# Second layer of a sparse two-layer graph network: tiles in a new order, all row gathers ahead of the accumulating output writes

## The chip, the cores and the metric

The kernel runs on one core of a Trainium2 chip. The metric is the device time of one execution in microseconds (us); less is better.

## What is computed

The input is x, 2048 rows of 512 numbers, and a random 0/1 matrix adj of 2048 x 2048 with about two ones in a row. The reference, cut:

```python
h = jnp.maximum(_layernorm(x, axis=-1), 0.0)
x = x + _L0_gnn_ref(h, adj, ...)   # 16 heads, scores only where adj is 1, projection, elu
h = jnp.maximum(_layernorm(x, axis=-1), 0.0)
x = x + _L1_gnn_ref(h, adj, ...)

def _L1_gnn_ref(sent_embed, adj_tensor, W_q, b_q, W_k, b_k, W_v, b_v):
    q = sent_embed @ W_q.T + b_q
    k = sent_embed @ W_k.T + b_k
    v = sent_embed @ W_v.T + b_v
    z = scale * (q @ k.T)
    spare_z = z * adj_tensor
    spare_z = jnp.where(spare_z == 0.0, -10000.0, spare_z)
    attn = jax.nn.softmax(spare_z, axis=1)
    return jax.nn.relu(attn @ v)
```

In the second layer every entry without an edge has the score -10000. So a row's attention is a common weight e0 for all 2048 rows plus corrections for its few neighbours.

## The kernel before, in words

**Ranking and tiles.** The kernel first sorts the 2048 rows by their number of neighbours and cuts them into 16 tiles of 128 rows. All rows of a tile have room for the same number of neighbours, the tile's *slots* (`SLOTS`). In the kernel's numbering tiles 0 to 3 have 1 slot each, tile 4 none, and tiles 5 to 15 have 8, 2, 5, 2, 4, 2, 3, 2, 3, 2, 3: 40 slots in all. A slot costs one *gather*: an indirect DMA, issued by GpSimd, that fetches for each of the tile's 128 rows one neighbour's row of 512 numbers.

**First layer.** It goes through the tiles in the order `SEQ`. For each, VectorE forms the hidden rows from gathered neighbours (`aggregate`), TensorE transposes and projects them, VectorE adds the input (`residual`, result in `x1[:, position, :]`), GpSimd takes the power for the normalisation (L1242) and writes x1 into the output tensor (L1243), and ScalarE makes the normalised rows `h_t` (L1115), which go to DRAM as `h1_dram` from the Sync queue (L1186). Between these steps GpSimd's queue issues gathers and loads of x by the tables `GATHER` and `X_LATE`. TensorE transposes h_t (L1334) and multiplies it with the joined query-key matrix: the *query products* (`queries`, L1344 and L1347), copied by ScalarE into `u_all` (`copy_u`).

**Second layer.** Six pieces per tile:

- GpSimd gathers the neighbours' normalised rows, one per slot (`gather1`, L1254). Where they land says `row(k)`: 20 places in `shared`, then 16 in `x1`, then `w_out`.
- VectorE forms one dot product per slot of u and the gathered row (`dot`, L985), then for a group of tiles the scores (`scores1`, L1004 to L1009); ScalarE exponentiates (`exp_scores1`, L1142 and L1143); VectorE normalises (`normalise1`, L1016 to L1023).
- ScalarE writes the *base row*, e0 times the sum of all normalised rows, into one of four buffers `hb` (`base_of`, L1135, for the tile without slots L1137, with the constant 1/N). It waits until the transposes of the tile four before have read that buffer.
- VectorE adds each gathered row times its weight to it (`aggregate1`, L1029, one instruction per slot).
- TensorE transposes the result (`transposes1`, L1388), ScalarE copies it (L1163), TensorE multiplies it with the value matrix into one of four banks (`products`, L1399 and L1401).
- ScalarE applies relu into one of four buffers `o_t` (`output`, L1150), and GpSimd adds these rows in DRAM to the output tensor, an accumulating indirect DMA, here called a *put* (`put`, L1259). ScalarE waits before it writes a buffer for the put that used it four tiles before.

The tiles come in the order 0 to 15, in the groups (0 to 4), (5, 6), (7, 8), (9, 10, 11), (12 to 15), and VectorE has a group's dot products behind the adds of the group before. Nothing schedules this work but the order in which it is written for each engine, each of which runs its instructions in order and waits on semaphores. On GpSimd stand nine tiles of gathers, then put and gathers by turns:

```python
for t in range(9):
    gather1(t)
for t in range(T):
    put(t)
    if 9 + t < T:
        gather1(9 + t)
```

## Time and profile before

| | us |
|---|---|
| median of 3 runs (lowest to highest) | 469.98 (469.42 to 470.12) |
| profiled execution, its own time | 469.46 |
| profiled execution, span from the first to the last instruction | 467.5 |
| TensorE busy | 395.3 (85%) |
| VectorE busy | 369.1 (79%) |
| ScalarE busy | 246.1 (53%) |
| GpSimd busy | 257.9 (55%) |

Of the span the first 205 us or so are the ranking, the input projections and the work on rows with no neighbour; the first layer's tile loop takes the next 140; the second layer runs from about 345 to the end. An engine's busy share is an average over these stages. In the profile PE is TensorE, DVE VectorE, ACT ScalarE, POOL GpSimd; L numbers are lines of the kernel.

### The profile page before, as it was taken

How to read it: one execution, taken by the hardware profiler on the slowest of the kernel's cores; microseconds unless marked ns; L12 is line 12 of the kernel's file. 1: busy time of each engine (PE TensorE's matmuls, PEld its weight loads, DVE VectorE, ACT ScalarE, POOL GpSimd, SP SyncE). 2: the span in 40 equal slices, each digit the busy share in tenths (PEclk: the TensorE clock that was granted, in tenths of full speed). 3: DMA queues.
4: the chain of work that ended last, by engine and by line, in shares of the span. 5: the costliest groups of instructions: out<-in, count | busy, mean ns of one | idle time of the engine just before them, and what ended most of it. 6: DMA issues, size and time to landing. Idle time of an engine off the chain costs nothing.

```text
span 467.5 us, 6241 instructions
## 1 busy us (share of the span) xinstructions
PE 395.3 (85%) x2058; PEld 282.6 (60%) x2070; DVE 369.1 (79%) x731; ACT 246.1 (53%) x511; POOL 257.9 (55%) x268
## 2 busy tenths in 40 slices
PE   7999999997899998989959879789891998866960
PEld 3888887784777887865737546456581565423430
DVE  4999999987899999977999996898445789957300
ACT  4389777766899998924424433444432433312310
POOL 2335241242788677766757648835337787871330
PEclk9599999999899999999989998899996899995995
DMA  8989998510000123445535527632136678873451
GB/s 315 399 320 332 390 339 299 201 70 2 6 6 5 23 72 92 104 126 182 188 87 166 162 91 205 197 122 91 46 113 192 199 174 168 165 162 43 52 65 19
DMA packets 26997, 70.02 MB, mean 150 GB/s; under 512 B 7893, under 2 KB 8149, under 8 KB 24789
## 3 DMA queue, kind: packets, MB, share of 16 engines
q0 software_dynamic: 13056, 38.45, 31.5%
q1 hardware_dynamic: 13904, 31.16, 18.3%
q8 instruction: 17, 0.28, 0.2%
q14 instruction: 16, 0.12, 0.1%
q10 hardware_dynamic: 4, 0.00, 0.0%
HBM read 52.47 MB, written 17.13 MB: 149 GB/s over the span
## 4 chain that ended last, share of the span: by engine, by line
POOL 31%; PE 15%; issue 15%; DVE 9%; DMA 1%; ACT 1%; DVEq 0%; POOLq 0%
PE psum L1303 8%; POOL s_shared L1231 7%; PE psum L1401 5%; POOL s_shared L1254 4%; POOL out_dram L1243 4%; POOL s_x L1254 4%; POOL s_shared L1212 3%; POOL s_rs L1242 3%; POOL out_dram L1259 3%; DVE s_shared L796 2%; DVE s_shared L794 2%; POOL s_x L1249 2%; DVE s_x L810 1%; DMA w_out<-h_dram,s_near_rank 1%; POOL w_out L1254 1%
## 5 line engine op out<-in xcount | busy, mean ns | idle before, releaser
L1064 ACT ACTIVATE s_shared<-psum,seq_all 128x320 bf16<-128x320 f32 x192 | 81.7, 568 | 6.1 <-PE psum L1303 4.4
L1303 PE MATMUL psum<-s_shared 128*128 128x198 bf16 x768 | 75.2, 254 | 9.6 <-POOL s_shared L1212 9.6
L1303 PEld LDWEIGHTS psum<-s_shared 128*128 128x128 bf16 x768 | 67.9, 98 | 17.4 <-POOL s_shared L1212 9.9
L555 PE MATMUL psum<-w_seq,hT 128*128 128x272 f32 x256 | 63.8, 405 | 0.4 <-ACT w_seq L416 0.4
L1325 PE MATMUL psum<-w_out,hT 128*128 128x512 f32 x128 | 60.7, 619 | 0.4
L555 PEld LDWEIGHTS psum<-w_seq,hT 128*128 128x128 f32 x256 | 49.4, 197 | 10.3 <-ACT w_seq L416 0.5
L1347 PE MATMUL psum<-w_qk,s_early 128*128 128x257 f32 x240 | 54.5, 379 | 0.0
L1347 PEld LDWEIGHTS psum<-w_qk,s_early 128*128 128x128 f32 x240 | 44.4, 190 | 6.0
L1231 POOL DMA_INDIRECT s_shared<-seq_dram,tab x30 | 37.7, 1255 | 11.3 <-issue 8.9
L1325 PEld LDWEIGHTS psum<-w_out,hT 128*128 128x128 f32 x128 | 26.0, 203 | 25.8 <-issue 24.9
L1212 POOL TENSOR_TENSOR s_shared<-s_shared 128x1056 f32<-128x1056 f32 x16 | 31.1, 1945 | 15.2 <-DVE s_shared L796 15.2
L274 POOL TENSOR_TENSOR rstd<-veps,power 128x1 f32<-128x1 f32 x16 | 8.9, 558 | 55.2 <-DVE veps L460 55.2
L472 DVE MAX8 near<-adj_ring 128x8 f32<-128x2048 f32 x16 | 36.5, 2284 | 0.6 <-DMA adj_ring<-in_adj_dram 0.6
L475 DVE FIND_INDEX8 tab<-near,adj_ring 128x8 uint32<-128x2048 f32 x16 | 36.6, 2285 | 0.0
L1242 POOL TENSOR_TENSOR s_rs<-s_ve,power 128x1 f32<-128x1 f32 x16 | 13.7, 855 | 38.7 <-DVE s_ve L898 38.6
L1115 ACT ACTIVATE h_t<-s_x,s_nm,s_rs 128x512 f32<-128x512 f32 x16 | 13.1, 816 | 36.5 <-DVE s_nm L905 36.5
L1401 PE MATMUL psum<-wv_t,hT 128*128 128x512 f32 x64 | 31.5, 639 | 0.8 <-ACT hT L1163 0.5
L1259 POOL DMA_INDIRECT out_dram<-s_lone,tab x12 | 19.4, 1619 | 20.6 <-ACT s_lone L1150 18.4
L803 DVE TENSOR_SCALAR s_shared<-psum,neg_s 128x320 bf16<-128x320 f32 x64 | 30.7, 541 | 0.0
L372 ACT ACTIVATE squares<-adj_ring 128x2048 bf16<-128x2048 f32 x16 | 30.4, 1897 | 0.0
L1401 PE MATMUL psum<-wv_t,bout_bc 128*128 128x512 f32 x64 | 28.8, 593 | 0.1
L1254 POOL DMA_INDIRECT s_shared<-h_dram,s_near_rank x20 | 20.6, 1028 | 9.0 <-issue 5.8
(264 smaller groups left out, 756.8 us busy)
## 6 DMA issues: line engine op xcount, KB each, us to landing
adj_ring<-in_adj_dram SPq DMA_DIRECT2D x16, 1024.0 KB, 8.1
seq_dram<-seq_all POOLq DMA_DIRECT2D x16, 264.0 KB, 4.7
x_ring<-in_x_dram SPq DMA_DIRECT2D x16, 256.0 KB, 8.4
h_dram<-h_t SPq DMA_DIRECT2D x16, 256.0 KB, 2.4
w_seq<-in_L_gnn_W_seq_dram SPq DMA_DIRECT2D x1, 1024.0 KB, 5.7
w_q<-in_L_gnn_W_q_dram SPq DMA_DIRECT2D x1, 1024.0 KB, 13.7
w_k<-in_L_gnn_W_k_dram SPq DMA_DIRECT2D x1, 1024.0 KB, 15.9
w_v<-in_L_gnn_W_v_dram SPq DMA_DIRECT2D x1, 1024.0 KB, 9.0
```

Source lines behind the costliest of these rows:

```text
L472: step(dve.max(near[:, t, :], adj_ring[:, t % AR, :]))
L475: dve.max_index(record[:, t, 0:TOP], near[:, t, :], adj_ring[:, t % AR, :]).then_inc(adj_searched, 1)
L555: last = pe.matmul(bank[2 + 2 * (t % 2) + i][:, 0:SX // 2], hT[:, t % 2, c * P:(c + 1) * P], w_seq[:, c, i * (SX // 2):(i + 1) * (SX // 2) ...
L1064: last = act.activation(ind[i][:, j, PAD:], bank[4 + i][:, 0:LN], ACT.Sign, bias=seq_all[:, j, D + n:D + n + 1])
L1212: pool.tensor_tensor(split[i][:, :, 2, :], split[i][:, :, 1, :], top_half(split[i][:, :, 1, :]), ALU.subtract).then_inc(r2_done, 1)
L1231: pool.indirect_dma_start(G(t)[:, s, :], None, seq_dram[:, :], bass.IndirectOffsetOnAxis(tab[:, t, s:s + 1], 0)).then_inc(got[t], 16)
L1254: pool.indirect_dma_start(row(FIRST_SLOT[t] + s), None, h1_dram[:, :], bass.IndirectOffsetOnAxis(near_rank[:, FIRST_SLOT[t] + s:FIRST_SLOT ...
L1259: pool.indirect_dma_start(out[:, :], bass.IndirectOffsetOnAxis(own[:, t, :], 0), o_t[t % 4], None, compute_op=ALU.add).then_inc(out_stored ...
L1303: last = pe.matmul(acc(i)[:, k, 0:3 * W2], ind[i][:, j, k * P:(k + 1) * P], rhs.rearrange("p t w -> p (t w)"), start=(j == 0 and k != 1), ...
L1325: last = pe.matmul(bank[2 + k % 2], hidT[k % 2][:, c * P:(c + 1) * P], w_out[:, c, :], start=False, stop=(c == C - 1))
L1347: last = pe.matmul(bank[u_bank(t) + i][:, 0:hi - lo], h1T(t)[:, c * P:(c + 1) * P], w_qk[:, c, lo:hi], start=False, stop=(c == C - 1))
L1401: last = pe.matmul(bank[2 + t % 4], aT[t % 2][:, c * P:(c + 1) * P], wv_t[:, c, :], start=False, stop=(c == C - 1))
```

## The change

Line numbers in this section are the changed kernel's where the text says so.

- **Tile order.** The second layer takes the tiles in the order `SEQ1` = 4, 0, 1, 2, 3, 6, 8, 10, 12, 14, 11, 13, 15, 9, 7, 5. The groups are now (0 to 3), (6, 8, 10), (12, 14), (9, 11, 13, 15), (5, 7). VectorE's order is written out by hand: dot products of later tiles stand between the adds of earlier ones.
- **GpSimd.** All 40 gathers stand ahead of all 16 puts, with one wait ahead of the 29th and one ahead of the 37th, whose targets are read by earlier work.
- **Places.** Gathered rows no longer use x1: 20 places in `shared`, 4 in `w_out`, 3 in `lone`, 1 in `bv_bc`, 8 in `early`, and the first four places again. ScalarE writes the relued rows into x1, at the tile's own position, and the puts read them there. The wait for an earlier put goes; instead ScalarE waits until all rows of x1 are stored. (`STORED` is 16, so `BY_DVE` is empty and every output goes this way.)
- **TensorE.** The query products of tiles 12 to 14 in `SEQ` order follow the sum of all normalised rows (before, one stood ahead of it, one behind, and the last two between the second layer's tiles); the last stands behind the first transposes. The banks of the query products alternate for all tiles.
- **ScalarE.** Exponentials, waits for weights and base rows are put by the tables `EXP1_AT`, `WEIGHTS_AT`, `BASES_AT`; an output now comes two tiles behind its copy, before one.
- **First layer.** GpSimd gathers 6 of tile 5's rows ahead of the tile loop instead of 5, and the table `GATHER` moves gathers of tiles 7, 9 and 11 one step forward.

```diff
-GATHER = {0: ((5, 5, 8),), 1: ((7, 0, 3),), 2: ((7, 3, 5),), 3: ((9, 0, 3),), 4: ((9, 3, 4), (11, 0, 2)),
-          5: ((11, 2, 3), (12, 0, 2)), 6: ((14, 0, 2),), 7: ((13, 0, 3),), 8: ((15, 0, 3),)}
-X_EARLY = 4
+GATHER = {0: ((5, 6, 8), (7, 0, 2)), 1: ((7, 2, 5),), 2: ((9, 0, 3),), 3: ((9, 3, 4), (11, 0, 2)), 4: ((11, 2, 3),),
+          5: ((12, 0, 2),), 6: ((14, 0, 2),), 7: ((13, 0, 3),), 8: ((15, 0, 3),)}
...
-U1_AT = {4: 14, 6: 15}
...
+SEQ1 = [4, 0, 1, 2, 3, 6, 8, 10, 12, 14, 11, 13, 15, 9, 7, 5]
+POS1 = {t: p for p, t in enumerate(SEQ1)}
+ROW1 = {t: sum(SLOTS[i] for i in SEQ1[:p]) for p, t in enumerate(SEQ1)}
+EXP1_AT = {2: 1, 4: 2, 8: 3, 11: 4}
+BASES_AT = {0: (1, 2, 3), 1: (4,), 3: (5, 6, 7), 5: (8, 9), 9: (10, 11, 12), 10: (13,), 12: (14, 15)}
+WEIGHTS_AT = {0: 1, 3: 2, 5: 3, 9: 4, 12: 5}
+STORED = T
+BY_ACT = [p for p in range(T) if TURN[SEQ1[p]] < STORED]
+BY_DVE = [p for p in range(T) if TURN[SEQ1[p]] >= STORED]
...
 
         def u_bank(t):
-            return 6 if t >= EARLY or U_NO[t] % 2 else 4
+            return 6 if U_NO[t] % 2 else 4
 
...
-        o_t = [lone[:, 0, :], lone[:, 1, :], lone[:, 2, :], bv_bc[:, :]]
...
-        PARTS = [(0, 4), (5, 2), (7, 2), (9, 3), (12, 4)]
-        first_of = {t0: g for g, (t0, n) in enumerate(PARTS)}
-        with_slots = [sum(n > 0 for n in SLOTS[:k]) for k in range(T + 1)]
+        PARTS = [slice(0, 4), slice(6, 11, 2), slice(12, T, 2), slice(9, T, 2), slice(5, 8, 2)]
+        PART_TILES = [len(range(T)[part]) for part in PARTS]
+        FIRSTS = (1,)
+        with_slots = [sum(SLOTS[t] > 0 for t in SEQ1[:p]) for p in range(T + 1)]
...
-        def row(k):
+        ROWS_EARLY = FLAT_ROWS + C + LONE + 1
+        ROWS_AGAIN = ROWS_EARLY + EARLY - 4
+
+        def row(t, s):
+            k = ROW1[t] + s
+            if k >= ROWS_AGAIN:
+                k -= ROWS_AGAIN
             if k < FLAT_ROWS:
                 return shared[:, k * D:(k + 1) * D]
-            if k < FLAT_ROWS + T:
-                return x1[:, k - FLAT_ROWS, :]
-            return w_out[:, k - FLAT_ROWS - T, :]
+            if k < FLAT_ROWS + C:
+                return w_out[:, k - FLAT_ROWS, :]
+            if k < FLAT_ROWS + C + LONE:
+                return lone[:, k - FLAT_ROWS - C, :]
+            if k < ROWS_EARLY:
+                return bv_bc[:, :]
+            return early[:, 4 + k - ROWS_EARLY, 0:D]
...
+                constants(0, EARLY)
                 dve.wait_ge(h_sum_mm, 1)
                 dve.tensor_copy(h_sum, bank[0]).then_inc(sums_ready, 1)
-                constants(0, EARLY)
+                for t in range(4):
+                    dot(t)
                 scores1(0)
+                dot(6)
                 normalise1(0)
...
-                for g in range(1, len(PARTS)):
-                    t0, n = PARTS[g]
-                    if g > 1:
-                        for t in range(PARTS[g - 1][0], t0 - 1):
-                            aggregate1(t)
-                    scores1(g)
-                    if g > 1:
-                        aggregate1(t0 - 1)
-                    normalise1(g)
-                for t in range(*(PARTS[-1][0], T)):
-                    aggregate1(t)
+                dot(8)
+                dot(10)
+                scores1(1)
+                constants(EARLY, T)
+                dot(12)
+                normalise1(1)
+                aggregate1(6)
+                dot(14)
+                scores1(2)
+                aggregate1(8)
+                normalise1(2)
+                aggregate1(10)
+                dot(11)
+                dot(13)
+                aggregate1(12)
+                dot(15)
+                dot(9)
+                aggregate1(14)
+                scores1(3)
+                dot(7)
+                normalise1(3)
+                aggregate1(11)
+                dot(5)
+                aggregate1(13)
+                scores1(4)
+                aggregate1(15)
+                normalise1(4)
+                aggregate1(9)
+                aggregate1(7)
+                aggregate1(5)
 
             @block.scalar
...
+                copy_h1T(T - 1)
                 copy_u(12)
-                copy_h1T(T - 1)
                 copy_u(13)
 
-                def base_of(t):
-                    if t >= 4:
-                        act.wait_ge(a_tr, t - 3)
+                def base_of(p):
+                    t = SEQ1[p]
+                    if p >= 4:
+                        act.wait_ge(a_tr, p - 3)
                     if SLOTS[t]:
-                        act.activation(hb[t % 4], h_sum, ACT.Copy, scale=e0[:, t:t + 1]).then_inc(base_ready, 1)
+                        act.activation(hb[p % 4], h_sum, ACT.Copy, scale=e0[:, t:t + 1]).then_inc(base_ready, 1)
                     else:
-                        act.activation(hb[t % 4], h_sum, ACT.Copy, scale=1.0 / N).then_inc(base_ready, 1)
+                        act.activation(hb[p % 4], h_sum, ACT.Copy, scale=1.0 / N).then_inc(base_ready, 1)
+
+                def output(p):
+                    act.wait_ge(o_done, p + 1)
+                    act.wait_ge(x1_stored, STORED * 16)
+                    act.activation(x1[:, TURN[SEQ1[p]], :], bank[2 + p % 4], ACT.Relu).then_inc(o_relu, 1)
...
                 act.wait_ge(sums_ready, 1)
-                act.wait_ge(none_set, 1)
                 for i in range(2):
                     act.wait_ge(h1_stored[i], T // 2 * 16)
+                base_of(0)
+                copy_u(14)
+                act.wait_ge(none_set, 1)
                 exp_scores1(0)
-                base_of(0)
-                base_of(1)
                 for k in range(T):
                     act.wait_ge(a_tr, k + 1)
                     if k >= 2:
                         act.wait_ge(o_done, k - 1)
                     act.activation(aT[k % 2], bank[k % 2], ACT.Copy).then_inc(aT_done, 1)
-                    if k + 2 < T:
-                        if k + 2 in first_of:
-                            exp_scores1(first_of[k + 2])
-                        base_of(k + 2)
-                    if k >= 1:
-                        output(k - 1)
-                    if k in U1_AT:
-                        copy_u(U1_AT[k])
-                output(T - 1)
+                    if k in EXP1_AT:
+                        exp_scores1(EXP1_AT[k])
+                    if k in WEIGHTS_AT:
+                        act.wait_ge(weights_ready, WEIGHTS_AT[k])
+                    for p in BASES_AT.get(k, ()):
+                        base_of(p)
+                    if k == 0:
+                        copy_u(15)
+                    if k - 2 in BY_ACT:
+                        output(k - 2)
+                for p in (T - 2, T - 1):
+                    if p in BY_ACT:
+                        output(p)
...
-                gather(5, 0, 5)
+                gather(5, 0, 6)
...
-                        pool.indirect_dma_start(row(FIRST_SLOT[t] + s), None, h1_dram[:, :],
+                        k = ROW1[t] + s
+                        if k == ROWS_EARLY:
+                            pool.wait_ge(u_done, U_NO[EARLY - 1] + 1)
+                        if k == ROWS_AGAIN:
+                            pool.wait_ge(agg_ready, 4)
+                        pool.indirect_dma_start(row(t, s), None, h1_dram[:, :],
                                                 bass.IndirectOffsetOnAxis(near_rank[:, FIRST_SLOT[t] + s:FIRST_SLOT[t] + s + 1], 0)).then_inc(got[t], 16)
-
-                def put(t):
-                    pool.wait_ge(o_ready, t + 1)
-                    pool.indirect_dma_start(out[:, :], bass.IndirectOffsetOnAxis(own[:, t, :], 0),
-                                            o_t[t % 4], None, compute_op=ALU.add).then_inc(out_stored[t % 4], 16)
 
                 pool.wait_ge(hid_ready, T - 2)
                 pool.wait_ge(summed, T)
-                pool.wait_ge(x1_stored, T * 16)
                 pool.wait_ge(proj_done, T)
+                pool.wait_ge(x1_stored, STORED * 16)
                 for i in range(2):
                     pool.wait_ge(h1_stored[i], T // 2 * 16)
-                for t in range(9):
+                for t in SEQ1:
                     gather1(t)
-                for t in range(T):
-                    put(t)
-                    if 9 + t < T:
-                        gather1(9 + t)
-                for i in range(4):
-                    pool.wait_ge(out_stored[i], T // 4 * 16)
...
+                for p in range(T):
+                    t = SEQ1[p]
...
+                    else:
+                        pool.wait_ge(o_relu, BY_ACT.index(p) + 1)
+                        pool.indirect_dma_start(out[:, :], bass.IndirectOffsetOnAxis(own[:, t, :], 0),
+                                                x1[:, TURN[t], :], None, compute_op=ALU.add).then_inc(out_stored, 16)
+                pool.wait_ge(out_stored, T * 16)
...
-                queries(12)
                 transposes_h1(T - 1)
                 pe.wait_ge(summed, T)
                 pe.wait_ge(hidT_done, T)
                 pe.matmul(bank[0], ones[:, 0:P], h_acc).then_inc(h_sum_mm, 1)
-                queries(13)
+                for t in range(EARLY, T - 1):
+                    queries(t)
...
-                        pe.wait_ge(o_ready, t - 3)
+                        if t - 4 in BY_DVE:
+                            pe.wait_ge(o_added, BY_DVE.index(t - 4) + 1)
+                        else:
+                            pe.wait_ge(o_relu, BY_ACT.index(t - 4) + 1)
                     elif t < 2:
                         pe.wait_ge(x1_ready, T)
                     else:
-                        pe.wait_ge(u_copied, U_NO[11] + 1)
+                        pe.wait_ge(u_copied, T - 1)
...
                 transposes1(0)
+                queries(T - 1)
                 for k in range(1, T):
-                    if k in first_of:
+                    if k in FIRSTS:
                         products(k - 1)
                         transposes1(k)
                     else:
                         transposes1(k)
                         products(k - 1)
-                    if k in U1_AT:
-                        queries(U1_AT[k])
```

How the instructions now stand. **GpSimd, second layer**; `s_shared`, `s_x`, `w_out`, `s_lone`, `bv_bc`, `s_early` are where gathered rows land, `out_0_dram` is the output tensor. Before, the first nine rows of the layer:

```order
L1254 DMA s_shared<-h_dram,s_near_rank 128x512 x20
L1254 DMA s_x<-h_dram,s_near_rank 128x512
L1259 DMA out_dram<-s_lone,tab 2048x512
L1254 DMA s_x<-h_dram,s_near_rank 128x512 x4
L1259 DMA out_dram<-s_lone,tab 2048x512
L1254 DMA s_x<-h_dram,s_near_rank 128x512 x2
L1259 DMA out_dram<-s_lone,tab 2048x512
L1254 DMA s_x<-h_dram,s_near_rank 128x512 x3
L1259 DMA out_dram<-bv_bc,tab 2048x512
```

and with the change, the whole layer:

```order
L1300 DMA s_shared<-h_dram,s_near_rank 128x512 x20
L1300 DMA w_out<-h_dram,s_near_rank 128x512 x4
L1300 DMA s_lone<-h_dram,s_near_rank 128x512 x3
L1300 DMA bv_bc<-h_dram,s_near_rank 128x512
L1300 DMA s_early<-h_dram,s_near_rank 128x512 x8
L1300 DMA s_shared<-h_dram,s_near_rank 128x512 x4
L1319 DMA out_dram<-s_x,tab 2048x512 x16
```

The 16 puts (L1259 before, L1319 now) have moved behind the last gather, and their source is x1.

**VectorE, end of the second layer**: the last group. Before (L1029 is the add of one gathered row, L1016 to L1023 normalise):

```order
L1029 SCALAR_TENSOR_TENSOR s_shared<-s_x,hT,s_shared 128x512 x3
L1016 TENSOR_TENSOR hT<-hT,s_others 128x4
L1017 TENSOR_REDUCE hT<-hT 128x4
L1018 TENSOR_TENSOR hT<-s_valid,hT 128x32
L1019 TENSOR_TENSOR hT<-hT 128x4
L1020 RECIPROCAL hT<-hT 128x4
L1021 TENSOR_TENSOR hT<-hT 128x4
L1022 TENSOR_TENSOR hT<-hT 128x32
L1023 TENSOR_TENSOR hT<-hT 128x32
L1029 SCALAR_TENSOR_TENSOR h_t<-s_x,hT,h_t 128x512 x5
L1029 SCALAR_TENSOR_TENSOR s_shared<-s_x,hT,s_shared 128x512
L1029 SCALAR_TENSOR_TENSOR s_shared<-w_out,hT,s_shared 128x512 x4
```

and with the change (L1044 is the add, L1030 to L1037 normalise):

```order
L1031 TENSOR_REDUCE hT<-hT 128x2
L1032 TENSOR_TENSOR hT<-s_valid,hT 128x2x8
L1033 TENSOR_TENSOR hT<-hT 128x2
L1034 RECIPROCAL hT<-hT 128x2
L1035 TENSOR_TENSOR hT<-hT 128x2
L1036 TENSOR_TENSOR hT<-hT 128x2x8
L1037 TENSOR_TENSOR hT<-hT 128x2x8
L1044 SCALAR_TENSOR_TENSOR h_t<-w_out,hT,h_t 128x512
L1044 SCALAR_TENSOR_TENSOR h_t<-s_lone,hT,h_t 128x512 x3
L1044 SCALAR_TENSOR_TENSOR s_shared<-bv_bc,hT,s_shared 128x512
L1044 SCALAR_TENSOR_TENSOR s_shared<-s_early,hT,s_shared 128x512 x8
L1044 SCALAR_TENSOR_TENSOR s_shared<-s_shared,hT 128x512 x4
```

Behind the last normalisation stood tiles 12 to 15 with 2, 3, 2 and 3 adds; now tiles 9, 7 and 5 with 4, 5 and 8.

**GpSimd, start of the first layer's loop** (DMA from `seq_dram` is a gather, L1242 before and L1282 now the power for the normalisation). Before:

```order
L1231 DMA s_shared<-seq_dram,tab 128x529 x5
L1242 TENSOR_TENSOR s_rs<-s_ve,power 128x1
L1243 DMA out_dram<-s_x,tab 2048x512
L1231 DMA s_shared<-seq_dram,tab 128x529 x3
L1249 DMA s_x<-in_x_dram,tab 128x512
```

and with the change:

```order
L1271 DMA s_shared<-seq_dram,tab 128x529 x6
L1282 TENSOR_TENSOR s_rs<-s_ve,power 128x1
L1284 DMA out_dram<-s_x,tab 2048x512
L1271 DMA s_shared<-seq_dram,tab 128x529 x4
L1290 DMA s_x<-in_x_dram,tab 128x512
```

Two more gathers stand ahead of the second power operation, one of them ahead of the first.

## Rows read from the trace of the kernel before

**Rows 1.** The page's head: span and number of instructions.

```profile
span 467.5 us, 6241 instructions
```

**Rows 2.** GpSimd's timeline, second layer: start us, us busy, instruction, count, [idle before <-releaser].

```profile
347.52 0.98 POOL L1254 DMA_INDIRECT s_shared<-h_dram,s_near_rank  x1 [3.25 <-DMA h_dram<-h_t]
...
375.44 1.64 POOL L1259 DMA_INDIRECT out_dram<-s_lone,tab  x1 [0.30 <-issue]
...
414.99 0.95 POOL L1254 DMA_INDIRECT w_out<-h_dram,s_near_rank  x1 [0.30 <-issue]
...
418.17 1.58 POOL L1259 DMA_INDIRECT out_dram<-s_lone,tab  x1 [0.30 <-issue]
```

**Rows 3.** The chain of waits near the end: start us, us, what.

```profile
414.99 4.13 DMA w_out<-h_dram,s_near_rank
...
453.34 1.55 POOL out_dram L1259
```

**Rows 4.** VectorE's timeline, second layer.

```profile
351.06 0.69 DVE L985 CUSTOM_DVE_ANT_0 w_seq<-seq_all,s_shared 128x512 f32<-128x512 f32 x1 [1.54 <-DMA s_shared<-h_dram,s_near_rank]
...
376.50 6.33 DVE L1029 SCALAR_TENSOR_TENSOR h_t<-s_shared,hT,h_t 128x512 f32<-128x512 f32 x8 [0.57 <-ACT h_t L1135]
...
395.45 0.69 DVE L985 CUSTOM_DVE_ANT_0 w_seq<-seq_all,s_x 128x512 f32<-128x512 f32 x1
...
400.45 0.68 DVE L985 CUSTOM_DVE_ANT_0 w_seq<-seq_all,s_x 128x512 f32<-128x512 f32 x1
...
401.17 0.18 DVE L1004 TENSOR_TENSOR hT<-hT 128x24 f32<-128x24 f32 x1
...
402.23 0.18 DVE L1009 TENSOR_TENSOR hT<-hT 128x24 f32<-128x24 f32 x1
...
403.78 0.15 DVE L1016 TENSOR_TENSOR hT<-hT,s_others 128x3 f32<-128x3 f32 x1
...
404.85 0.18 DVE L1023 TENSOR_TENSOR hT<-hT 128x24 f32<-128x24 f32 x1
...
419.15 0.69 DVE L985 CUSTOM_DVE_ANT_0 w_seq<-seq_all,w_out 128x512 f32<-128x512 f32 x1 [4.68 <-DMA w_out<-h_dram,s_near_rank]
```

**Rows 5.** TensorE's timeline, second layer.

```profile
343.19 0.39 PE L1344 MATMUL psum<-bias_rows,ones_b 128*128 128x257 bf16 x2
...
346.88 0.60 PE L1334 MATMUL psum<-ident,h_t 128*128 128x128 f32 x4
...
424.99 1.11 PE L1388 MATMUL psum<-ident,s_shared 128*128 128x128 f32 x4 [8.17 <-DVE s_shared L1029]
...
426.33 5.56 PE L1401 MATMUL psum<-wv_t,hT 128*128 128x512 f32 x8
...
440.32 0.60 PE L1388 MATMUL psum<-ident,s_shared 128*128 128x128 f32 x4
...
444.41 0.60 PE L1388 MATMUL psum<-ident,s_shared 128*128 128x128 f32 x4
```

**Rows 6.** Accesses of the output tensor, 346 to 468: time to landing.

```profile
DMA to landing us min/median/max: 4.8/5.0/5.6
```

**Rows 7.** GpSimd's instructions in groups, 375 to 415: busy us, mean ns | idle before.

```profile
L1259 POOL DMA_INDIRECT out_dram<-s_lone,tab x6 | 10.1, 1680 | 1.8 <-issue 1.8
```

**Rows 8.** Two windows of 2 us: busy time by engine, granted clock, DMA share, GB/s.

```profile
425.00:427.00 2.00, 2.00 (x6) 1.51 (x7) 1.33 (x9) 1.15 (x3) 0.00 (x0) 0.50 0.00 0
431.00:433.00 2.00, 2.00 (x7) 0.92 (x6) 0.00 (x0) 0.60 (x1) 0.20 (x1) 1.00 0.30 53
```

**Rows 9.** First layer, timelines of GpSimd and VectorE.

```profile
220.28 0.58 POOL L1242 TENSOR_TENSOR s_rs<-s_ve,power 128x1 f32<-128x1 f32 x1
...
230.87 4.34 POOL L1231 DMA_INDIRECT s_shared<-seq_dram,tab  x1 [0.31 <-issue]
...
222.21 0.17 DVE L837 COPY s_near_rank<-s_shared 128x8 uint32<-128x8 uint32 x1 [0.93 <-DMA s_shared<-seq_dram,tab]
...
229.95 4.42 DVE L876 TENSOR_TENSOR s_shared<-s_shared,s_sc 128x4096 f32<-128x4096 f32 x1
```

65 lines of the change are left out of this document (31 added, 34 removed).

## The prediction

> **What bounds the kernel now.** I read four views: the page for the span, the chain of waits for what sets the end, and the timelines of the engines for the second layer, about a quarter of the 467.5 us [rows 1]. The chain shows three pieces. The row gathers of the second layer start at 347.52, released by the DMA that puts the last normalised tile into DRAM [rows 2]. From there to 414.99 the chain lies on GpSimd's queue (POOL): 40 gathers of neighbour rows, with seven accumulating output writes ("puts") between them. The last gather lands 4.13 us later [rows 3], VectorE (DVE) had waited 4.68 us for it [rows 4], and TensorE (PE), which had waited 8.17 us, then works off the last six products [rows 5]. The last put is issued at 453.34 [rows 3], and the span ends 14.16 later: landing, 4.8 to 5.6 us [rows 6], and the end of the program, which no edit touches. So two things cost time: puts ahead of gathers, and PE work that piles up behind the last ones.
>
> **Durations.** 21 gathers lie between 347.52 and the first put at 375.44, 1.33 us each. From there to 414.99 are 7 puts and 18 gathers after the first put; a put takes 1.58 us busy and 0.30 idle in the row at 418.17, and 1.68 busy on the mean among the gathers [rows 2, 7], so seven cost 7 x 2.0 = 14.0. The other (414.99 - 375.44 - 14.0)/18 = 1.42 us is a gather beside a busy DVE. A dot product, (400.45 - 395.45)/8 = 0.625. One weighted add, 6.33/8 = 0.79. The six small score operations, from 401.17 to 402.23 plus 0.18: 1.24, and 0.11 before them. The eight of the normalisation, 403.78 to 404.85 plus 0.18: 1.25 [rows 4]. PE per tile, 444.41 - 440.32 = 4.09; one tile's query product, 346.88 - 343.19 = 3.69 [rows 5].
>
> **The change, by its parts.**
>
> 1. *All gathers ahead of all puts.* The first gather still waits for the same DRAM write. The last starts after 21 x 1.33 + 18 x 1.42 = 53.5 us, at 401.0 instead of 414.99. The seven puts are 14.0 us of that. The two new waits in the gather queue cost nothing. The one before row 29 asks for the query product that ends at 343.19 [rows 5], and the one before row 37, near 396, for the first four aggregated tiles, which DVE has near 367.
>
> 2. *Longest tiles last, positions on DVE.* Tile 5 (8 slots) is gathered last, and its eight dots wait for the last row. I walked DVE's new order with the durations above. It starts at 351.06 [rows 4], has 40 dots, 40 adds and five rounds of scores and normalising, 25.0 + 31.6 + 13.0 = 70 us, and waits about 8 us: the first gathers, the base rows, and 2.8 for PE, whose queries now stand before the first transposes. It would be ready for tile 5 near 403, and the last row lands at 401.0 + 4.13 = 405.1. Before, DVE had 4 dots behind its last row; now it has 8 dots (5.0), scores (1.35), normalising (1.25), and the adds of tiles 13, 15, 9, 7 and 5, 3 + 3 + 4 + 5 + 8 = 23 (18.2): 25.8 in all, to 430.9.
>
> 3. *PE starts earlier and has little left at the end.* The tile without slots needs no scores, so PE goes from the queries straight on. Its floor is 4 x 3.69 + 16 x 4.09 = 80.2 us from about 346 (the product before these ends at 343.19 [rows 5]; the last normalised tile and the sum follow), so 426.2, below DVE's 430.9: PE no longer sets the end, it waits. Behind the last add are only the last transposes and two products. The same piece ended the kernel before: from the transposes at 444.41 to the put at 453.34 are 8.93 us [rows 3, 5]. The last put starts at 430.9 + 0.1 + 8.9 = 439.9.
>
> 4. *Sixteen puts in a row.* They can begin at 402.4. At 2.0 us, twelve are out by 426.4, and from there each waits for its tile: nothing is added while the put pitch is under (439.9 - 402.4)/15 = 2.5. The new targets (the tiles' own rows of x1) remove ScalarE's wait for an earlier put, which was met in time anyway: nothing. The writes land in 5.0 us [rows 6] and overlap: the put at 418.17 was issued 1.9 us after another.
>
> 5. *PE's clock.* The waits that my walk leaves before PE's tenth and eleventh transposes are some 4.5 us each. Before, after the 8.17 us wait, the granted clock was 0.50 from 425 to 427 and 1.00 from 431 on [rows 8]: 1.2 and 2.4 GHz. The product at 426.33 took 5.56 instead of some 3.6 [rows 5], so a drop costs about 2.4 us with its transposes. The first falls into PE's own next wait and is hidden. The second delays the transposes that free the buffers for the last tiles, which in my walk come about 2 us before DVE asks for them. I count 0.5, between 0 and 4.8. **The Trainium skill** (TensorE: Matmul & The Clock Gate, Part 1) says the throttled clock is the default and activity releases it. If by that page both waits cost their whole drop, the sum would be about 4 us more.
>
> 6. *First layer.* One more gather of tile 5 stands ahead of the loop and two of tile 7's in step 0: 11 transfers up to the end of step 0 instead of 9. The rstd of step 1 ran at 220.28 right behind the queue [rows 9] and now comes two transfers, some 2.5 us, later; DVE's operation on it ends near 223.7. DVE waited until 222.21 for tile 5's last row in any case [rows 9], and that row now comes about 1.3 earlier. So DVE loses about 1.5, and I find no slack that takes all of it back. I count 1.3, between -0.5 and 3.
>
> **Sum.** 439.9 + 0.5 + 1.3 = 441.7; plus 14.16 is a span of 455.9 instead of 467.5. The profiled execution took 469.46, 1.96 more than its span, and the median of the runs is 469.98. So 457.8, about 12 below. **I predict 457.5 us**; own range 453 to 462.
>
> **Rivals.**
>
> *Smaller gain.* The gathers now run without a pause while DVE is almost always busy. For: the pitch rose from 1.33 to 1.42 when DVE filled up. If it goes on to 1.6 throughout, the last gather starts at 409.9, 9 us later, and everything behind it too: 466.5. Both clock drops (4.8) and a first layer longer by 3 would give 457.5 - 1.8 + 7.8 = 463.5. Against: 18 gathers beside a busy DVE are in the 1.42.
>
> *Larger gain.* First-layer delay absorbed and gathers at 1.33: the last row lands at 403.5 and DVE is free at 403, so 1.6 + 1.3 + 0.5 = 3.4 less; with 0.5 gained in the first layer, 453.6. Below 453 the base waits would have to vanish too.
>
> *Slower, by the port.* At 230.87 a gather took 4.34 us beside one DVE operation of 4.42 us at 229.95 [rows 9]. If every gather were held for one DVE operation of about 0.75, the pitch would be 0.95 + 0.30 + 0.75 = 2.0, the last gather would start at 425.5, 24.5 late, and the kernel would take 482. It decides from a pitch of 1.7: (470 - 457.5)/39 = 0.32 above the mean of 1.37. Against: the kernel before had the same dots and adds beside its gathers and reached 1.42. **The Trainium skill** (SBUF — State Buffer, the section on ports) has this as a rule: VectorE and GpSimd share a port pair under an exclusive lock, and an operation with two SBUF inputs holds it against a GpSimd operation that reads SBUF. The stalled gather agrees, the pitch in the second layer does not show it.
>
> *Slower, by the puts.* If accumulating writes queue for each other's landing, 5.0 us each [rows 6], the last of sixteen starts at 402.4 + 75 = 477.4: 495. It decides from a pitch of 3.4. Against: puts 1.9 us apart landed in the usual time.
>
> *The change does nothing.* That would need the last gather not to bind before; the 4.68 us wait of DVE [rows 4] says it does.
>
> **How the numbers follow.** My forecast 0.70; smaller gain 0.16; larger gain 0.08; slower by the port 0.03, by the puts 0.02; gain used up and no difference 0.01. A difference under 0.2% (0.9 us) can't be told from none here. Faster: 0.94; same 0.01; slower 0.05. The range 451 to 465 leaves out the slower cases, half of the smaller gain, and little at the low end.
>
> **What would show it.** Last gather starting at 401 +- 3, pitch 1.3 to 1.45. DVE waiting about 2 us or less before tile 5's dots, and its last add ending near 431 to 433. PE from about 358 without a wait over 1 us until 395, then two waits of 3 to 5. About 8.9 us from the last transposes to the last put, which waits for ScalarE. First gather at 348 to 349. I am wrong if DVE waits several times for gathers, if the puts are still back to back at the end, or if DVE has idle stretches behind ScalarE's base rows that I put at 0.3 us each: ScalarE now copies, exponentiates and writes outputs in one fixed order, and a late one of these is next in line.

## The result and the profile after

| us | before | changed |
|---|---|---|
| median (lowest to highest) | 469.70 of 4 (468.36 to 470.12) | 451.91 of 4 (451.39 to 453.11) |
| profiled execution, span | 467.5 | 450.1 |
| last put starts | 453.34 | 436.38 |

The ratio is 0.963, 95% interval 0.9602 to 0.9657: 17.8 us less. The forecast was 457.5 with a range of 451 to 465; the narrower own range of the prediction, 453 to 462, is missed by 1.1 us. This holds for the occasion on which it was measured. On a later one, shown below, the same kernel was slower than the one before.

The page's head and busy times of the changed kernel, where [rows 1] had a span of 467.5:

```profile
span 450.1 us, 6244 instructions
...
PE 393.3 (87%) x2058; PEld 281.5 (63%) x2070; DVE 368.4 (82%) x731; ACT 245.7 (55%) x511; POOL 255.9 (57%) x268
```

GpSimd's timeline in the second layer; the first gather, the last one, the first put and the last put answer to [rows 2, 3]:

```profile
347.00 0.98 POOL L1300 DMA_INDIRECT s_shared<-h_dram,s_near_rank  x1 [3.24 <-DMA h_dram<-h_t]
...
397.98 0.95 POOL L1300 DMA_INDIRECT s_shared<-h_dram,s_near_rank  x1 [0.30 <-issue]
399.24 1.64 POOL L1319 DMA_INDIRECT out_dram<-s_x,tab  x1 [0.30 <-issue]
...
436.38 1.55 POOL L1319 DMA_INDIRECT out_dram<-s_x,tab  x1 [2.04 <-ACT s_x L1180]
```

The 40 gathers now stand in a row and the last starts at 397.98 instead of 414.99, 17.01 us earlier. The last put starts 16.96 us earlier. The chain of waits ends the gathers with the same kind of row as before:

```profile
397.98 4.38 DMA s_shared<-h_dram,s_near_rank
...
436.38 1.55 POOL out_dram L1319
```

VectorE: its first dot product, its longest wait within the layer, its wait for the last row (which answers to 419.15 in [rows 4]), and its last four adds:

```profile
350.49 0.69 DVE L1003 CUSTOM_DVE_ANT_0 w_seq<-seq_all,s_shared 128x512 f32<-128x512 f32 x1 [4.20 <-DMA s_shared<-h_dram,s_near_rank]
...
366.07 0.75 DVE L1044 SCALAR_TENSOR_TENSOR h_t<-s_shared,hT,h_t 128x512 f32<-128x512 f32 x1 [3.10 <-ACT h_t L1173]
...
402.38 0.69 DVE L1003 CUSTOM_DVE_ANT_0 w_seq<-seq_all,s_early 128x512 f32<-128x512 f32 x1 [0.84 <-DMA s_shared<-h_dram,s_near_rank]
...
424.23 3.11 DVE L1044 SCALAR_TENSOR_TENSOR s_shared<-s_shared,hT 128x512 f32<-128x512 f32 x4
```

TensorE's three waits, the product behind the first, and the last product ([rows 5]):

```profile
401.60 0.79 PE L1434 MATMUL psum<-ident,s_shared 128*128 128x128 f32 x4 [3.69 <-DVE s_shared L1044]
...
402.61 4.98 PE L1450 MATMUL psum<-wv_t,bout_bc 128*128 128x512 f32 x8
409.67 0.66 PE L1434 MATMUL psum<-ident,s_shared 128*128 128x128 f32 x4 [2.08 <-DVE s_shared L1044]
...
427.39 0.66 PE L1434 MATMUL psum<-ident,s_shared 128*128 128x128 f32 x4 [1.17 <-DVE s_shared L1044]
...
431.75 3.60 PE L1450 MATMUL psum<-wv_t,bout_bc 128*128 128x512 f32 x8
```

The windows show busy times of PE, PEld, DVE, ACT and POOL, granted clock, DMA share and GB/s; the first is a stretch of the gathers, the others answer to [rows 8]:

```profile
385.00:390.00 5.00, 5.00 (x19) 2.66 (x18) 4.96 (x15) 1.09 (x2) 3.96 (x4) 1.00 0.68 213
402.00:406.00 4.00, 4.00 (x9) 1.97 (x8) 3.62 (x11) 1.70 (x3) 3.39 (x3) 0.58 0.98 127
409.00:413.00 4.00, 3.33 (x12) 1.86 (x13) 3.76 (x12) 1.37 (x4) 3.47 (x2) 1.00 1.01 128
```

The last row is there when VectorE starts on it at 402.38. 24.97 us later, at 427.35, VectorE is done. TensorE's last transposes start at 427.39 and the last put at 436.38, 8.99 later. 13.72 us follow to the end of the span.

Of the first layer, GpSimd's second power and VectorE's operation behind it ([rows 9]), and the gather that stood 4.34 us there:

```profile
221.16 0.59 POOL L1282 TENSOR_TENSOR s_rs<-s_ve,power 128x1 f32<-128x1 f32 x1
...
230.54 4.34 POOL L1271 DMA_INDIRECT s_shared<-seq_dram,tab  x1 [0.31 <-issue]
```

```profile
221.78 0.16 DVE L923 SCALAR_TENSOR_TENSOR s_nm<-s_mv,s_rs 128x1 f32<-128x1 f32 x1 [0.95 <-POOL s_rs L1282]
221.86 0.16 DVE L855 COPY s_near_rank<-s_shared 128x8 uint32<-128x8 uint32 x1
...
229.63 4.42 DVE L894 TENSOR_TENSOR s_shared<-s_shared,s_sc 128x4096 f32<-128x4096 f32 x1
```

### The profile page after: what moved, and what is told of

Its sections match the earlier page's. It is cut to its first block, busy times and chain, and to the rows that moved or that the text cites. A ratio compares the mean times of both kernels' runs of the same rounds, so it can differ in the third digit from the quotient of the medians.

```text
span 450.1 us, 6244 instructions
## 1 busy us (share of the span) xinstructions
PE 393.3 (87%) x2058; PEld 281.5 (63%) x2070; DVE 368.4 (82%) x731; ACT 245.7 (55%) x511; POOL 255.9 (57%) x268
## 4 chain that ended last, share of the span: by engine, by line
POOL 28%; DVE 16%; issue 15%; PE 11%; DMA 2%; ACT 1%; DVEq 0%; POOLq 0%
PE psum L1349 7%; POOL s_shared L1271 7%; POOL s_shared L1300 5%; POOL out_dram L1284 4%; POOL s_shared L1252 3%; POOL s_rs L1282 3%; DVE s_shared L814 3%; DVE s_shared L812 3%; DVE s_shared L1044 3%; POOL s_x L1290 2%; POOL s_early L1300 2%; PE psum L1450 2%; DVE s_x L828 2%; DVE s_shared L821 1%; DVE h_t L1044 1%
## 5 line engine op out<-in xcount | busy, mean ns | idle before, releaser
L1282 POOL TENSOR_TENSOR s_rs<-s_ve,power 128x1 f32<-128x1 f32 x16 | 13.6, 850 | 39.1 <-DVE s_ve L916 39.0
L1319 POOL DMA_INDIRECT out_dram<-s_x,tab x16 | 27.0, 1685 | 12.0 <-ACT s_x L1180 8.7
L1450 PE MATMUL psum<-wv_t,bout_bc 128*128 128x512 f32 x64 | 30.2, 616 | 0.0
L1300 POOL DMA_INDIRECT s_shared<-h_dram,s_near_rank x24 | 24.1, 1004 | 10.3 <-issue 7.0
L1450 PE MATMUL psum<-wv_t,hT 128*128 128x512 f32 x64 | 28.8, 592 | 0.2
```

The costliest lines, as they stand in the source:

```text
L1300: pool.indirect_dma_start(row(t, s), None, h1_dram[:, :], bass.IndirectOffsetOnAxis(near_rank[:, FIRST_SLOT[t] + s:FIRST_SLOT[t] + s + 1], ...
L1450: last = pe.matmul(bank[2 + t % 4], aT[t % 2][:, c * P:(c + 1) * P], wv_t[:, c, :], start=False, stop=(c == C - 1))
```

## The experiments

They ran on four occasions, each beside the kernel before: it took 476.37 us at the first four runs, 476.43 at the next four, 468.82 at the two after, 476.93 at the last two. So ten of the twelve were measured when both kernels were slower than in the result. I call those ten disturbed and say below what the disturbance looks like; a difference between a disturbed and an undisturbed run says nothing on an edit. The record also has a chip number for each of the four: 0, 0, 8 and 1. So the two undisturbed runs were the only ones on chip 8; which chip the result came from is not recorded.

### The changed kernel once more

> The changed kernel itself, as the comparison for the three runs beside it: 451.9 within 0.5.

Measured: 485.35 us (484.86 to 486.84), ratio to the kernel before 1.0195 (1.0148 to 1.0242). The change costs 9 us here instead of bringing 17.8. The traces of the two executions of the same program show where. TensorE's last query product in this one, starting at 359.19 with 3.64 us:

```profile
359.19 3.64 PE L1393 MATMUL psum<-w_qk,s_early 128*128 128x257 f32 x16
```

ScalarE waits for its end (third line), and before that for the ends of the query product and of the transposes ahead of it (first and second line; their modelled ends are 3.4 and 8.6 us earlier):

```profile
362.06 0.39 ACT L1120 ACTIVATE seq_all<-psum 128x257 f32<-128x257 f32 x1 [5.84 <-remote]
...
367.75 0.60 ACT L1199 ACTIVATE hT<-psum 128x512 f32<-128x512 f32 x1 [4.74 <-remote]
...
400.11 0.39 ACT L1120 ACTIVATE seq_all<-psum 128x257 f32<-128x257 f32 x1 [29.93 <-remote]
```

The product's modelled end is 362.83, and ScalarE's copy of it starts at 400.11, 37.3 us later. "remote" says that the profile finds nobody who ended the wait. Since the ends of matmuls are modelled, the trace can't tell a late signal from matmuls that end late; "late signal" below stands for either. Everything else stands behind that: VectorE's fourth aggregated tile comes at 401.89, so GpSimd waits 7.67 us with the 37th gather, whose place is read by it, and for ten us no engine but GpSimd works, while DMA goes on as ever:

```profile
401.89 0.75 DVE L1044 SCALAR_TENSOR_TENSOR h_t<-s_shared,hT,h_t 128x512 f32<-128x512 f32 x1 [30.75 <-ACT h_t L1173]
```

```profile
394.29 0.96 POOL L1300 DMA_INDIRECT s_early<-h_dram,s_near_rank  x1 [0.30 <-issue]
402.92 1.16 POOL L1300 DMA_INDIRECT s_shared<-h_dram,s_near_rank  x1 [7.67 <-DVE h_t L1044]
```

```profile
385.00:395.00 10.00, 0.00 (x0) 0.00 (x0) 0.00 (x0) 0.00 (x0) 7.56 (x9) 0.50 0.68 210
```

In the undisturbed trace that copy came at 361.9, no wait of ScalarE was "remote", and between 350 and 398 TensorE was busy 47.5 of 48 us. GpSimd's own pitch is not disturbed, 1.26 us just ahead of its wait.

### Puts between the gathers

```diff
# in short
-for t in SEQ1: gather1(t)
-for p in range(T): put(p)
+for n, (t, s) in enumerate(rows of SEQ1):
+    if n in (20, 23, 26, 29, 32, 35, 38): put(next)
+    gather1(t, s)
+then the other nine puts
```

> The changed kernel, but with seven of the sixteen output writes on GpSimd's queue between the last 20 gathers, as the kernel before had them. The tile order, places and all else stay. Theory A: each put holds the queue for 2.0 us (the prediction) to 2.29 us (worked out from the changed kernel's gather pitch of 1.307), so the last gather starts 14 to 16 us later, at 412 to 414, and the kernel takes 466 to 468: all of the gain but 2 to 4 us is gone. Theory B, the new tile order brings the gain: under 458. For the prediction's 1.42 us, a gather beside a busy VectorE: the gathers directly behind a put take over 1.0 us in this run if it was the puts that slowed them, and all stay at 0.95 if not.

> The changed kernel with seven puts between the last gathers, once more. Undisturbed (kernel before near 469, TensorE's signals on time): Theory A, the puts hold the queue, last gather start 412 to 414 and 466 to 468. Theory B, the tile order brings the gain: under 458. A price of 2.0 us a put gives 466, one of 2.29 us gives 468. Disturbed as in its first run: 477 to 480.

Measured, both disturbed: 478.93 us, ratio 1.0061 (1.0027 to 1.0095), and 477.76, ratio 1.0029 (1.001 to 1.0048). GpSimd's, ScalarE's and VectorE's timelines of the second:

```profile
371.88 0.96 POOL L1300 DMA_INDIRECT s_shared<-h_dram,s_near_rank  x1 [0.30 <-issue]
382.98 1.95 POOL L1311 DMA_INDIRECT out_dram<-s_x,tab  x1 [10.14 <-ACT s_x L1180]
385.24 1.00 POOL L1300 DMA_INDIRECT w_out<-h_dram,s_near_rank  x1 [0.30 <-issue]
...
422.22 0.96 POOL L1300 DMA_INDIRECT s_shared<-h_dram,s_near_rank  x1 [0.30 <-issue]
...
461.47 1.55 POOL L1311 DMA_INDIRECT out_dram<-s_x,tab  x1 [2.04 <-ACT s_x L1180]
```

```profile
375.51 0.39 ACT L1120 ACTIVATE seq_all<-psum 128x257 f32<-128x257 f32 x1 [7.58 <-remote]
```

```profile
426.62 0.69 DVE L1003 CUSTOM_DVE_ANT_0 w_seq<-seq_all,s_early 128x512 f32<-128x512 f32 x1 [9.21 <-DMA s_shared<-h_dram,s_near_rank]
```

Three things can be read. The first put waits 10.14 us for its output, behind ScalarE's wait for TensorE until 375.51; that alone makes the last gather some 10 us late. From that put to the last gather, 39.24 us, lie 7 puts and 19 gathers; the distances behind the seven puts add up to 13.83, so **a put takes 1.98 us of the queue** and a gather 25.41 / 19 = 1.34. Theory A's price of 2.0 holds and 2.29 falls. And the end follows the last row: from VectorE's start on it, 426.62, to the last put, 461.47, are 34.85 us, where the changed kernel has 436.38 - 402.38 = 34.00. Without the wait, seven puts would cost 13.8 us plus 20 x 0.03. Added to 451.9 that is an estimate of some 466 for this kernel undisturbed, which was not measured.

On the gathers directly behind a put the expectation named two outcomes, all over 1.0 us or all at 0.95. Neither came: six of the seven took 0.98 to 1.00 and one 1.50.

The last thing: behind the first put, where puts and gathers alternate, ScalarE has no "remote" wait any more.

### Pauses in the gathers

```diff
 for t in SEQ1:
     gather1(t)
+    if t in (10, 13, 7):
+        pool.wait_ge(got[t], 32 * SLOTS[t])
```

> In the eight runs so far the changed kernel took 485 us and the kernel before 476, instead of 451.9 and 469.7. Their traces show why in the place, not in the cause: TensorE's semaphore for a finished product reaches ScalarE up to 37 us after the modelled end of the matmuls, and the last of them comes at 400.1, 2.3 us behind the last packet of the first 36 gathers (397.8). This run is the changed kernel with GpSimd waiting three times, after rows 10, 20 and 32, until the last row has landed, which makes three pauses of about 3.1 us in the gathers. Theory A, the signals are held up while gathers follow each other without a pause: where the runs beside it are disturbed as before, ScalarE's waits end in the pauses, near 360 to 363, 375 to 379 and 393 to 397, none is over 20 us, and the kernel is faster than the changed one by 10 us or more: under 475. Theory B, the delay has nothing to do with the gathers: 485 + 9 = 494. If this run is undisturbed, the theory that the gather queue bounds the second layer gives 451.9 + 3 x 3.1 = 461, less VectorE's 0.84 of waiting for the last row: 460 to 461.5; if VectorE or TensorE bound it, under 456.

Measured, undisturbed: 465.35 us (461.86 to 465.6), ratio 0.9885 (0.9843 to 0.9928). No ScalarE wait is "remote", so this run says nothing on the disturbance, but it is the test of the bound. The first gather, the row behind each pause, the last gather and the last put, VectorE's wait for the last row and a later one, and a window of TensorE's:

```profile
348.20 0.99 POOL L1300 DMA_INDIRECT s_shared<-h_dram,s_near_rank  x1 [3.25 <-DMA h_dram<-h_t]
...
364.22 0.95 POOL L1300 DMA_INDIRECT s_shared<-h_dram,s_near_rank  x1 [3.05 <-DMA s_shared<-h_dram,s_near_rank]
...
380.52 1.02 POOL L1300 DMA_INDIRECT w_out<-h_dram,s_near_rank  x1 [2.90 <-DMA s_shared<-h_dram,s_near_rank]
...
399.31 1.28 POOL L1300 DMA_INDIRECT s_early<-h_dram,s_near_rank  x1 [3.61 <-DMA s_early<-h_dram,s_near_rank]
...
408.73 0.95 POOL L1300 DMA_INDIRECT s_shared<-h_dram,s_near_rank  x1 [0.30 <-issue]
...
449.55 1.55 POOL L1321 DMA_INDIRECT out_dram<-s_x,tab  x1 [2.04 <-ACT s_x L1180]
```

```profile
414.06 0.69 DVE L1003 CUSTOM_DVE_ANT_0 w_seq<-seq_all,s_early 128x512 f32<-128x512 f32 x1 [7.72 <-DMA s_shared<-h_dram,s_near_rank]
...
430.23 0.76 DVE L1044 SCALAR_TENSOR_TENSOR s_shared<-bv_bc,hT,s_shared 128x512 f32<-128x512 f32 x1 [1.05 <-ACT s_shared L1173]
```

```profile
421.00:425.00 4.00, 3.66 (x8) 2.20 (x9) 3.76 (x12) 1.37 (x4) 3.24 (x3) 0.50 1.04 148
```

The expected 460 to 461.5 was 4 us short of the median. The five executions fall in two groups, 461.86 and 462.18 against 465.35 to 465.6; the first nearly meets it. What follows is the trace of one of the slower three, and why two were faster is open. The last put is 449.55 - 436.38 = 13.17 us later than in the changed kernel, and it splits without rest: first gather 1.20 later (348.20); from it to the last gather 60.53 instead of 50.98, so 9.55 more, of which the pauses are 3.05 + 2.90 + 3.61 less their usual 0.30 each, 8.66; the last row 0.93 slower to arrive; and 35.49 instead of 34.00 behind it, 1.49. Of these 1.49, 1.05 are the wait at 430.23. TensorE had waited 8.82 us before, its clock was at 1.2 GHz (0.50), its product took 5.84 instead of 3.60, the transposes that free a buffer came late, and with them ScalarE's base row. So all of the gathers' delay reached the end: theory A's bound holds, and the others, which gave under 456, fall, by the faster group too. What is shown is that a delay of the gathers reaches the end; that less delay would bring as much is not.

### Base row earlier, dot products in halves

```diff
-BASES_AT = {0: (1, 2, 3), 1: (4,), 3: ...
+BASES_AT = {0: (1, 2, 3, 4), 3: ...
...
-dot(5)
+dot(5, 0, 4)
 aggregate1(13)
+dot(5, 4, TOP)   # each half has a semaphore of its own
```

> The changed kernel with the base row of the fifth tile of the order moved ahead of ScalarE's next copy, which takes away VectorE's wait of 3.10 us at 366.07. Theory A, the gather queue bounds the second layer: VectorE's wait for the last row grows from 0.84 to 3 to 4 us, and the end stays: 451.9 within 0.4. Theory B, VectorE bounds it: the 3.10 us come off the end, 448.8. Theory C: ScalarE or TensorE lose by the new order what VectorE gains, 452.5 or more, with a new wait on TensorE before 365.

> The changed kernel with the last gathered tile's eight dot products in two halves, each waiting for its own four rows. VectorE waits 0.84 us for the last row in the changed kernel and has four dot products, 2.5 us, to do in that time now. Theory A, the last row and VectorE's work behind it set the end: the wait goes and 0.84 comes off, 451.1 (450.7 to 451.5), and nothing more, since VectorE is then busy without a break. Theory B, TensorE sets the end: its wait of 1.17 before the last transposes is longer than 0.84, so it could not: no difference at 451.9 would mean that VectorE's operations get slower instead.

> Both edits (base row earlier, last tile's dot products in two halves) and the adds of tile 13 between the halves. Theory A, gathers and VectorE bind nearly equally: with VectorE 3.10 us ahead and only four dot products behind the last row, VectorE ends 3.9 us earlier, at 423.4, TensorE sets the end then, at its pace of 4.09 us per tile from 403.3: last transposes at about 423.7, 3.7 less: 448.2 (447.3 to 449.3). Theory B, the gather queue alone: as with the halves alone, 451.1. Theory C, VectorE alone: 448.8 with the base row moved alone and no more here.

> The version with the base row earlier, the last tile's dot products in halves and the adds of tile 13 between them, once more. Undisturbed: 448.2 (447.3 to 449.3), as worked out before. Disturbed as in its first run: 478 to 491, with ScalarE waiting for TensorE until the gathers end.

Measured, disturbed: base row alone 490.32 (476.96 to 490.83), halves alone (without the changed place of tile 13's adds) 484.41 (479.61 to 486.0), both 489.38 (477.83 to 490.99). These say nothing on the theories: ScalarE waits 29.68, 21.78 and 22.49 us at a time for TensorE in them. The disturbance differs between executions of one kernel too: those of the first and of the third lie 13 to 14 us apart. Both edits undisturbed: 450.02 us (448.35 to 450.31), ratio 0.9589 (0.9559 to 0.9619). That is 1.9 less than the changed kernel's 451.91, but the two ratios' intervals touch, so a gain over it is likely and not established. Its trace shows why it is not the expected 3.7:

```profile
393.05 0.69 DVE L1009 CUSTOM_DVE_ANT_0 w_seq<-seq_all,bv_bc 128x512 f32<-128x512 f32 x1 [1.28 <-DMA s_early<-h_dram,s_near_rank]
```

```profile
398.64 0.96 POOL L1307 DMA_INDIRECT s_shared<-h_dram,s_near_rank  x1 [0.30 <-issue]
...
434.24 1.55 POOL L1326 DMA_INDIRECT out_dram<-s_x,tab  x1 [2.04 <-ACT s_x L1187]
```

VectorE no longer waits 3.10 us for the base row and has no wait for the last row, but 3.10 earlier it comes to a row that is not there yet and waits 1.28 for it, at 393.05, and 0.20 more for a base row before. The last gather starts at 398.64, 0.66 later than in the changed kernel, and the last put at 434.24, 2.14 earlier. The measured 450.02 lies between the 451.1 of the gather queue alone and the 448.8 of VectorE alone, and meets none of the three forecasts. By the trace gathers and VectorE bind by turns, and what one of them is given the other takes in part.

### The old tile order, the old first layer, and the kernel before with its puts last

```diff
-SEQ1 = [4, 0, 1, 2, 3, 6, 8, 10, 12, 14, 11, 13, 15, 9, 7, 5]
+SEQ1 = list(range(T))    # and groups, exponentials, base rows, VectorE's order as before;
+                         # the last query product ahead of the first transposes
```

> The changed kernel with the tiles in the order 0 to 15, the old groups and the old order of VectorE's work, but all gathers ahead of the puts and outputs in x1. Theory A, the queue's order is nearly all of the gain and the tile order a small part: VectorE waits for tile 5's eight rows near the start, some 5 us, which the gathers can't give back since VectorE has 70 us of work, and TensorE starts its tiles later: 455 to 461. Theory B, the tile order is most of the gain: over 464. Theory C, the tile order brings nothing: under 453.

> The changed kernel with the old tile order and groups, once more. Undisturbed: 455 to 461 if the tile order is a small part of the gain (VectorE waits some 5 us for tile 5's eight rows near the start), over 464 if it is most of it, under 453 if it is nothing. Disturbed as in its first run: 492 to 496.

```diff
-GATHER = {0: ((5, 6, 8), (7, 0, 2)), 1: ((7, 2, 5),), ...
+GATHER = {0: ((5, 5, 8),), 1: ((7, 0, 3),), 2: ((7, 3, 5),), ...
-gather(5, 0, 6)
+gather(5, 0, 5)
```

> The changed kernel with the first layer's gathers as before (five rows of tile 5 ahead of the loop, the old table). The first gather of the second layer started 0.52 us earlier in the changed kernel (347.00 against 347.52), of which 0.38 is there already ahead of the first layer's loop. Theory A: the moved gathers give the small rest, 0.1 to 0.2 us; the run takes the changed kernel's time, 451.9, within 0.4, and its first gather starts at 347.0 to 347.3. Theory B, the prediction's step: the moved gathers cost 1.3 us, hidden in the comparison by something else; then this run takes about 450.6. Theory C: they bring what the prediction missed, over 1 us: 453 or more.

```diff
 # the kernel before
-for t in range(9): gather1(t)
-for t in range(T):
-    put(t)
-    if 9 + t < T: gather1(9 + t)
+for t in range(T): gather1(t)
+for t in range(T): put(t)
```

> The kernel before with one edit: all forty gathers ahead of all sixteen puts, the four output buffers as they were. Theory A: ScalarE's fifth output waits for the first put, which now comes at 399 and lands at 404, and all of ScalarE's work behind it stands from about 385 on; TensorE has eleven products left at 404: 404 + 11 x 4.09 + 2 + 14 = 465, at most 475. So the new places, not the queue's order alone, make the gain. Theory B, the step of the prediction by which the removed wait for an earlier put is worth nothing holds here too: as with the old tile order, 455 to 461.

Measured, all disturbed: old order 494.97 and 495.76, ratios 1.039 and 1.0409; old first layer 485.47, ratio 1.0171 (1.0138 to 1.0204); kernel before with puts last 493.35, ratio 1.0355 (1.0303 to 1.0406).

The old first layer takes the time of the changed kernel, 485.35, within the spread; the two stand on neighbouring occasions, so the medians can't tell 1.3 us. The traces can. The distance from the first gather of tile 5 in the first layer (204.36 in the changed kernel, 204.74 before, 205.74 here) to the first gather of the second layer is 142.77 us in this run, 142.78 in the kernel before and 142.43 in its version with the puts last: the three with the old table. With the new table it is 142.64 in the changed kernel and 142.55 to 142.85 in nine other traces; only the second run of the changed kernel has 144.51, and lost its time between 315 and 330, far behind the moved gathers. So the moved gathers cost nothing that can be seen, at most 0.4 us either way: theory A holds, without its 0.1 to 0.2, and B (1.3 us lost) and C (over 1 us gained) fall.

The old order takes 10 us more beside the same disturbance, more than the 5 expected, but VectorE's long waits in it (15.37 and 14.02 us in the first run, 13.44 and 19.63 in the second) come from TensorE's late signals, so what the tile order is worth undisturbed stays open. In the kernel before with its puts last, ScalarE's wait was not the expected one. It is its second output, and the next put stands right behind it:

```profile
397.10 0.96 POOL L1254 DMA_INDIRECT w_out<-h_dram,s_near_rank  x1 [0.30 <-issue]
398.36 1.64 POOL L1259 DMA_INDIRECT out_dram<-s_lone,tab  x1 [0.31 <-issue]
405.90 1.58 POOL L1259 DMA_INDIRECT out_dram<-s_lone,tab  x1 [5.90 <-ACT s_lone L1150]
```

```profile
404.90 0.60 ACT L1150 ACTIVATE s_lone<-psum 128x512 f32<-128x512 f32 x1 [20.61 <-remote]
```

The fifth output, which has to wait for the first put, comes later, so the question of the four buffers stays open too. But this run tells of the disturbance: 17 us more than the kernel before beside it, by one edit, which puts the 40 gathers in a row.

## Why the prediction was right, point by point

The mechanism was right: the gathers set the end, and taking the puts from between them moved it. In the kernel before, the distances behind the seven puts ahead of the last gather add up to 14.06 us, of the 17.01 by which that gather moved. The size was too small, though: 12 us forecast, 17.8 measured. The last put came at 436.38 instead of the forecast 441.7, 5.3 us earlier. To that the gathers' pitch gave 2.5, the first layer's term that was not paid 1.3, VectorE's shorter work 0.8, an earlier start of the second layer 0.5 and the clock's term 0.5; the last row's slower arrival took 0.3 back. How much of the gain is the new tile order's is not shown, since both runs with the old order were disturbed.

**Step 1, all gathers ahead of all puts.** Right in kind: last gather at 397.98, forecast 401.0. The puts' 2.0 us each was right (1.98 measured). The two new waits in the queue cost nothing here, as forecast; the second cost 7.67 us in the disturbed run. The term that failed is "1.42 us is a gather beside a busy DVE". In the window of 385 to 390 VectorE is busy 4.96 of 5 us, and most gathers take 0.95; the 39 distances have a mean of (397.98 - 347.00) / 39 = 1.307 instead of 1.37: 2.5 us. What made 1.42 of it in the kernel before is not shown: in the disturbed run with puts between them, gathers took 1.34.

**Step 2, longest tiles last.** The last row came 4.40 us behind its gather's start (4.13 assumed) and was read from 402.38, and VectorE was free at 401.54; forecast 405.1 and 403. Its work behind the last row took 24.97 instead of 25.8. VectorE's slack was 0.84 us and not 2, so both nearly bind, as the run with both edits shows. From VectorE's start on the last row to the last put it was 34.19 us before and 34.00 now. Before, TensorE's six products filled that time; now VectorE's work does. The prediction read four dot products behind the last row before; there were three (419.15 to 420.99), and none of its sums uses the four.

**Step 3, TensorE has little left.** 8.99 us from the last transposes to the last put, forecast 8.93. It waited 3.69, 2.08 and 1.17 us, where two waits of 3 to 5 were named.

**Step 4, sixteen puts in a row.** Back to back they started at most 2.24 us apart, and the last four waited for ScalarE, so they added nothing. "The wait for an earlier put, met in time anyway: nothing" holds for the kernel before: in its trace each wait of ScalarE ahead of an output, where there is one, ended with TensorE. It can't be carried over to the new order. There ScalarE writes the fifth output at 382.53 and the first put starts at 399.24, so with four buffers it would have had to wait some 17 us and the landing besides (worked out, not measured). So it is the outputs' own places in x1 that keep this wait away when all puts stand at the end.

**Step 5, TensorE's clock.** 0.5 us counted, none paid. One drop only (0.58 from 402 to 406, the product took 4.98), hidden by TensorE's next wait. The other wait, of 2.08, was followed by a clock of 1.00. So the sum by **the Trainium skill** (TensorE: Matmul & The Clock Gate, Part 1), with a drop paid for both waits, was too high by all of its 4 us; that an idle engine falls back to the throttled clock, its rule, agrees with the first wait (3.69 us, then 0.58). The way in which the step said that a drop reaches the end was seen in the run with pauses, at 1.05 us.

**Step 6, first layer.** The term was 1.3 us and should have been nothing. The second layer's first gather came 0.52 earlier (347.00 against 347.52), but 0.38 of that is there ahead of the loop, where no gather was moved. That first gather of tile 5 starts between 204.36 and 205.89 in the fourteen traces, so 0.52 is within what executions differ by. The time between the two starts, given above, is the same with both tables. The step said that DVE loses about 1.5 behind a power that comes two transfers later. One of the two was absorbed by 1.65 us for which GpSimd had waited before the loop's first power; with the 0.38 that the changed kernel was ahead before it, the second power came at 221.16 instead of 220.28. VectorE then waited 0.95 for it and no longer for tile 5's row, where it had waited 0.93: one wait took the place of the other.

The rest is the 0.44 us by which the end behind the last put was shorter, and 0.08 less outside the span.

**The rivals.** Slower by the port: the pitch of 1.307 beside a VectorE that is busy all the time excludes it for this layer. **The Trainium skill** (SBUF — State Buffer, section "SBUF: two separate sides") has VectorE's operations with two SBUF inputs hold off a GpSimd operation that reads SBUF for their whole length. The second layer doesn't show that for gathers; the first does, and not only at the place that the prediction names. The changed kernel's three gathers beside long VectorE operations took 4.34, 2.55 and 1.99 us (operations of 4.42, 2.82 and 2.28), and each ended 0.83 to 0.85 us behind the operation. Slower by the puts: 1.9 us apart they ran on. Larger gain: this is what came, though it had a chance of 0.08: gathers at 1.31, and no delay in the first layer. It went 1.6 us further than its 453.6, by VectorE's shorter work behind the last row and the shorter end.

**What no rival held.** On other occasions the change loses 9 us, by signals of TensorE that come late.

## What to carry to other kernels

Find the queue whose last item the end follows, and take everything out of it that can go behind: each put between gathers cost its full 1.98 us. When two engines bind nearly equally (0.84 us here), expect less than the sum from a further edit: 3.7 us were expected here and about 1.9 came. And measure such a change on more than one occasion, and on more than one chip: the order without a gap that won 17.8 us lost 9 when the chip was disturbed, while the kernel with puts between its gathers lost only 7 of its own time.
